# Rebuilding an attention core: transposed scores, row maxima one block ahead, every beat written out

## The reference

```
q, k, v = x @ Wq.T, x @ Wk.T, x @ Wv.T     # 32 query heads of 16, 16 key heads of 16, 8 value heads of 32
q, k = rope(q) * 16 ** -0.5, rope(k)       # each key head serves two query heads
probs = softmax(causal(q @ k.T))           # 32 maps of 1024 x 1024 for each sequence
diff = probs[even] - lambda * probs[odd]   # 16 differences; lambda from four small vectors
attn = rms_norm(diff @ v) * subln * (1 - LAMBDA_INIT)
x = x + attn @ Wo.T
h = gelu(layernorm(x) @ ternary(w1).T + b1)  # 512 -> 2048, weights -1, 0, 1
x = x + h @ ternary(w2).T + b2
```

## Time and profile before

| what | value |
| --- | --- |
| median of 3 runs | 4434.35 us (4434.32 to 4440.61) |
| span of the profiled execution | 4427.3 us |
| busy PE / DVE / ACT / POOL | 81 / 78 / 66 / 33% |
| HBM traffic | 106 MB read, 55 MB written |

### The profile page before, as it was taken

One profiled execution on the slowest core, in us unless ns is written; L12 is line 12 of the kernel. 1 busy time (PEld: TensorE's weight loads), 2 busy tenths in 40 slices (PEclk: granted clock), 3 DMA queues, 4 the chain that ended last, 5 costly groups with the idle time before them and its releaser, 6 DMA issues.

```text
span 4427.3 us, 80970 instructions
## 1 busy us (share of the span) xinstructions
PE 3604.6 (81%) x23454; PEld 2143.3 (48%) x23454; DVE 3467.0 (78%) x6124; ACT 2909.6 (66%) x6786; POOL 1450.2 (33%) x1563
## 2 busy tenths in 40 slices
PE   2688888888788887888878988888878888888886
PEld 1345544455444554544544544455544555444553
DVE  6778877888678886788867887678877788678891
ACT  1567756677566775667756766567666677567772
POOL 0233233332333333323343323433133332333323
PEclk7789989999899899998899988999989899899898
DMA  4212112211122112112122120222112121222110
GB/s 131 51 24 43 24 43 43 38 24 30 38 43 43 22 34 48 37 32 38 25 43 43 30 37 20 44 41 43 24 41 43 24 40 24 43 43 41 21 37 14
DMA packets 146768, 166.71 MB, mean 38 GB/s; under 512 B 16640, under 2 KB 117632, under 8 KB 145792
## 3 DMA queue, kind: packets, MB, share of 16 engines
q1 hardware_dynamic: 146304, 161.13, 18.0%
HBM read 105.95 MB, written 55.12 MB: 36 GB/s over the span
## 4 chain that ended last, share of the span: by engine, by line
PE 35%; DVE 28%; issue 22%; ACT 8%; DMA 3%; SPq 2%; POOL 2%; DVEq 1%; ACTq 0%; POOLq 0%
DVE NM L665 10%; PE M L867 6%; PE M L817 6%; PE F L889 5%; PE SP_ L832 5%; PE DP L844 5%; DVE E L689 4%; DVE CC L686 3%; PE F L902 3%; ACT E L541 2%; DMA KST<-scratch 2%; PE M L811 2%; ACT L541 2%; DVE RS L684 1%; DVE NM L673 1%
## 5 line engine op out<-in xcount | busy, mean ns | idle before, releaser
L541 ACT ACTIVATE E<-SP_,NM 128x256 f32<-128x256 f32 (+7 forms) x2048 | 1518.6, 743 | 733.6 <-DVE NM L665 526.4
L665 DVE TENSOR_REDUCE NM<-SP_ 128x1 f32<-128x896 f32 (+3 forms) x1024 | 1032.6, 1017 | 225.1 <-PE SP_ L833 222.9
L832 PE MATMUL SP_<-KST,QST 96*128 96x512 bf16 (+3 forms) x3072 | 864.1, 355 | 407.7 <-ACT E L541 345.5
L689 DVE SCALAR_TENSOR_TENSOR E<-E,CC 128x512 f32<-128x512 f32 (+7 forms) x1024 | 994.6, 971 | 36.1
L553 ACT ACTIVATE DT<-DP 128x512 f32<-128x512 f32 (+3 forms) x1024 | 527.8, 515 | 546.2 <-PE DP L844 524.0
L844 PE MATMUL DP<-ident,E 128*128 128x128 f32 x3328 | 614.5, 302 | 208.6 <-DVE E L689 207.3
L673 DVE TENSOR_REDUCE NM<-SP_ 128x2 f32<-128x1024 f32 (+3 forms) x512 | 419.8, 820 | 297.2 <-PE SP_ L833 290.3
L832 PEld LDWEIGHTS SP_<-KST,QST 96*128 96x128 bf16 x3072 | 278.7, 103 | 762.7 <-ACT E L541 537.1
L844 PEld LDWEIGHTS DP<-ident,E 128*128 128x128 f32 x3328 | 391.1, 153 | 382.2 <-issue 203.1
L889 PE MATMUL F<-X2H,W1Q 128*128 128x256 f16 x2048 | 502.0, 283 | 69.9 <-ACT HP L596 65.8
L817 PE MATMUL M<-WQKV,WT 128*128 128x512 f32 x1040 | 530.8, 607 | 8.4 <-DVE T L648 4.1
(11 more groups left out here) (86 smaller groups left out, 4780.3 us busy)
## 6 DMA issues: line engine op xcount, KB each, us to landing
QST<-scratch SPq DMA_DIRECT2D x390, 128.0 KB, 4.4
scratch<-SPL SPq DMA_DIRECT2D x65, 576.0 KB, 2.8
KST<-scratch SPq DMA_DIRECT2D x390, 64.0 KB, 5.0
X<-in_x SPq DMA_DIRECT2D x66, 256.0 KB, 3.1
out<-SQ SPq DMA_DIRECT2D x64, 256.0 KB, 2.1
KST<-in_w1T SPq DMA_DIRECT2D x1, 4096.0 KB, 19.2
DT<-in_w2T SPq DMA_DIRECT2D x1, 4096.0 KB, 28.7
WQKV<-in_wqT SPq DMA_DIRECT2D x1, 1024.0 KB, 7.3
```

Source lines behind the costliest of these rows:

```text
L541: act.activation(dst, score_out(i, 2 * n + k, w), ACT.Exp, bias=NM[:, (2 * u + k) % 8:(2 * u + k) % 8 + 1], scale=1.0, accum_out=SUM[:, i ...
L665: nc.vector.tensor_reduce(NM[:, m:m + 1], score_out(i, 2 * n + k, P * (i + 1)), AX.X, ALU.max, negate=True).then_inc(max_ready, 1)
L689: nc.vector.scalar_tensor_tensor(out=E1[:, u % 2, 0:w], in0=E2[:, e:e + w], scalar=CC[:, u % 2:u % 2 + 1], in1=E1[:, u % 2, 0:w], op0=ALU. ...
L832: pe.matmul(SP_[:, k[a // 512], 0:n], q, KST[0:ROWS, a // P:(a + n) // P, kk, :], start=True, stop=not last)
```

## The change

The attention core is written anew, and the order of work around it too.

- Scores are computed twice. `maxima` computes them with queries on the partitions, for the block after the current one (128 to 512 columns for each of two row halves of the array, 48 rows each), and VectorE reduces them to negative maxima, 152 reductions for each sequence of eight blocks. The maxima are turned by a transpose (`MT0`, `MT1`), cut to fp16 rows (`MROW`) and copied by eight small DMAs for each block into row 48 of `QST`; row 48 of `KST` holds ones. `scores_turned` then computes scores with keys on the partitions, with the negative maximum added by that row, in steps of eight heads (4 x 256 columns).
- ScalarE takes exp of 128 x 1024 in one instruction (`exps`), with no bias and no row sum. The result `PT` is already turned, and multiplies V directly (`weighted` on PE). Row sums come from a product with ones. There are 4 (t + 1) such steps for a block, in four phases.
- VectorE's `weighted` takes the reciprocal of 128 x 256 sums, multiplies, and forms the difference of the two maps after the V product, once for each phase.
- q and k are two fp16 parts with three products (48 rows) in place of three bf16 parts with six (96 rows). The projections are fp16 pairs: three fp16 matmuls in place of one f32.
- All work outside attention (projections, transposes, FFN products) goes through one bank `M`, one task for each of 16 beats of a block, with `m_full` and `m_free` as the only counters. First products: three pieces in odd blocks, five in even ones; second products: two in odd blocks. Projections run two blocks ahead, LN1 three.
- Nothing loops: all 64 blocks and 7 of start and tail are written out. The ternary weights are cut inside blocks -2 and 0.

```diff
-PROD = 6
-QPART = (0, 0, 0, 1, 1, 2)
-KPART = (0, 1, 2, 0, 1, 0)
+PROD = 3
+QPART = (0, 2, 1)
+KPART = (0, 1, 2)
+KEYS = 12
+BEATS = 16
+XT, AT, MT1, QP, KV, AN, QT, KT, WO_, MT0, X2T = 0, 2, 3, 4, 6, 8, 9, 11, 12, 13, 14
+FIRST_ODD, FIRST_EVEN = (1, 5, 7), (1, 5, 7, 10, 15)
+SECOND_ODD = (10, 15)
+SPLIT_ODD, SPLIT_EVEN = (1, 2, 6, 8), (6, 8, 9, 11)
+SQ_AT, MS_AT, POW_AT, MUL_AT = 3, 4, 5, 6
+ADD_Q, ADD_K, SPLIT_Q, SPLIT_K = 5, 7, 10, 12
+LN1_STATS, LN1_POW, LN1_ROWS = 10, 11, 15
+LN2_STATS, LN2_POW, LN2_ROWS = 12, 12, 13
+def group_at(n, k):
+    t = n % TILES
+    per = (t + 2) // 2
+    g = -(-k * 4 * per // BEATS)
+    if g >= 4 * per or g * BEATS // (4 * per) != k:
         return None
+    return g // per, 2 * (g % per), min(2 * (g % per) + 2, t + 1)
+def weighted_at(n, k):
+    m = n if k else n - 1
+    g = group_at(m, (k - 1) % BEATS)
+    return (m, *g) if g else None
+MAX_UNITS = (2, 4, 8, 8, 10, 12, 16, 16)
...
         @block.sync
...
+            def max_rows(n, u, blk, k):
+                m_taken(sp, blk, k)
+                for a in range(2):
+                    row = QST[64 * a + ROWS:64 * a + ROWS + 1, n % 3, :, :].rearrange("p (y c) n -> p y c n", c=4)
+                    for c2 in range(2):
+                        sp.dma_start(row[:, :, 2 * u + c2, :], MROW[8 * a + 4 * c2:8 * a + 4 * c2 + 4, u, :]).then_inc(rows_in[u], 16)
+            for n in range(-3, N + 4):
...
+                if tile(n + 2):
+                    stack_out(n + 2)
+                if tile(n + 1):
+                    max_rows(n + 1, 0, n, MT0)
+                if tile(n + 2):
+                    stack_in(n + 2)
...
         @block.scalar
...
+            def exps(n, ph, j0, j1):
+                for j in range(j0, j1):
+                    s = steps_before(n) + ph * (n % TILES + 1) + j
+                    after(act, st_full, s + 1)
+                    after(act, pv_done, s - 3)
+                    act.activation(PT[:, s % 4, :], STB[:, 2 * (s % 2):2 * (s % 2) + 2, :].rearrange("p a n -> p (a n)"),
+                                   ACT.Exp).then_inc(e_done, 1)
...
         @block.vector
...
+                after(dve, s_full, units_before(n, u) + i + 1)
+                nc.vector.tensor_reduce(dst, SB[:, :, 0:c * w].rearrange("p a (c w) -> p a c w", c=c), AX.X, ALU.max,
+                                        negate=True).then_inc(s_free, 1)
...
+            def weighted(n, ph):
+                f = 4 * n + ph
+                after(dve, pv_done, steps_before(n) + (ph + 1) * (n % TILES + 1))
+                nc.vector.reciprocal(RS[:, :], A[:, 2 * P:4 * P]).then_inc(inv_ready, 1)
+                after(dve, inv_ready, f + 1)
+                nc.vector.tensor_tensor(OD[:, :], A[:, 0:2 * P], RS[:, :], ALU.mult).then_inc(a_free, 1)
+                after(dve, a_free, f + 1)
+                nc.vector.scalar_tensor_tensor(out=ATC[:, n % 2, ph, :], in0=OD[:, P:2 * P], scalar=neglam[:, 0:1], in1=OD[:, 0:P],
+                                               op0=ALU.mult, op1=ALU.add).then_inc(at_ready, 1)
...
         @block.tensor
...
+                for j in range(j0, j1):
+                    s = steps_before(n) + ph * (t + 1) + j
+                    after(pe, e_done, s - 1)
+                    for c2 in range(2):
+                        for a in range(2):
+                            r = slice(64 * a, 64 * a + ROWS + 1)
+                            ins = pe.matmul(STB[:, 2 * (s % 2) + a, 256 * c2:256 * c2 + 256],
+                                            KST[r, (n - t + j) % KEYS, 2 * (2 * c2 + h2) + u, :],
+                                            queries(n)[r, 2 * h2:2 * h2 + 2, 2 * u + c2, :],
+                                            start=(c2 == 0), stop=(c2 == 1 and j < t), skip_group_check=True)
...
+                    after(pe, e_done, s + 1)
+                    if j == 0:
+                        after(pe, a_free, 4 * n + ph)
+                    for part in range(2):
+                        for c2 in range(2):
+                            for a in range(2):
+                                g = 2 * c2 + a
+                                v = DV * (4 * u + g)
+                                left = ones[:, 0:DV] if part else V[:, (n - t + j) % KEYS, v:v + DV]
+                                ins = pe.matmul(A[DV * g:DV * g + DV, 256 * part:256 * part + 256], left,
+                                                PT[:, s % 4, 512 * a + 256 * c2:512 * a + 256 * c2 + 256],
+                                                start=(part == 0 and j == 0), stop=(j == t), skip_group_check=True)
...
+            def maxima(n, u, i):
+                if u == 0 and i == 0:
+                    after(pe, stacked, STACK * (n + 1))
+                after(pe, s_free, units_before(n, u) + i)
+                for e in range(c):
+                    c2, y = divmod(e0 + e, 4)
+                    for a in range(2):
+                        r = slice(64 * a, 64 * a + ROWS)
+                        k1 = (n - t + k0) % KEYS
+                        ins = pe.matmul(SB[:, a, w * e:w * e + w], queries(n)[r, y, 2 * u + c2, :],
+                                        KST[r, k1:k1 + kt, 2 * (2 * c2 + y // 2) + u, :], start=(e == 0),
+                                        stop=(e == c - 1 and not diagonal), skip_group_check=True)
...
+            def project(high, low, wh, wl, c0):
+                for j in range(KD):
+                    c = slice(P * j, P * (j + 1))
+                    pe.matmul(M[:, :], high[:, c], wh[:, j, c0:c0 + D], start=(j == 0), stop=False)
+                    pe.matmul(M[:, :], high[:, c], wl[:, j, c0:c0 + D], start=False, stop=False)
+                    ins = pe.matmul(M[:, :], low[:, c], wh[:, j, c0:c0 + D], start=False, stop=(j == KD - 1))
+                ins.then_inc(m_full, 1)
...
+            for n in range(-3, N + 4):
+                for k in range(BEATS):
+                    if group_at(n, k):
+                        scores_turned(n, *group_at(n, k))
+                    u, units = units_at(n + 1, k)
+                    for i in units[:1]:
+                        maxima(n + 1, u, i)
+                    if weighted_at(n, k):
+                        weighted(*weighted_at(n, k))
+                    for i in units[1:]:
+                        maxima(n + 1, u, i)
+                    if (n, k) not in M_AT:
+                        continue
+                    after(pe, m_free, M_AT[n, k])
+                    if k == XT:
+                        after(pe, xn_ready, n + 3)
+                        turn(XN, KD)
...
+                    elif first_piece(n, k):
+                        after(pe, cut_done, 2)
+                        first_product(*first_piece(n, k))
+                    elif second_piece(n, k):
+                        second_product(*second_piece(n, k))
```

More of the change, by code:

```diff
@@ L169, in every_block @@
-def every_block(eng, run):
-    for t in range(TILES):
-        run(QBlock(0, t, "first"))
-    with eng.Fori(1, B) as b:
-        for t in range(TILES):
-            run(QBlock(b, t, "loop"))
-    for t in range(3):
-        run(QBlock(B, t, "last"))
+AS, WS = 32.0, 256.0
+PS = 1.0 / (AS * WS)
+LOW = 64.0
+PROD = 3
+QPART = (0, 2, 1)
+KPART = (0, 1, 2)
+ROWS = PROD * DH
+STACK = 4 * PROD * 16
+KEYS = 12
+BEATS = 16
+CUT = 1024
+XT, AT, MT1, QP, KV, AN, QT, KT, WO_, MT0, X2T = 0, 2, 3, 4, 6, 8, 9, 11, 12, 13, 14
@@ new lines, in joins_before, with units_before, units_at, unit @@
+def joins_before(n):
+    b, t = divmod(n, TILES)
+    return b * 8 + 2 * max(0, t - 4)
+MAX_UNITS = (2, 4, 8, 8, 10, 12, 16, 16)
+ABREAST = (4, 2, 1, 1)
+def units_before(n, u):
+    b, t = divmod(max(0, min(n, N)), TILES)
+    return b * 2 * sum(MAX_UNITS) + 2 * sum(MAX_UNITS[:t]) + u * MAX_UNITS[t]
+def units_at(n, k):
+    if not tile(n):
+        return 0, range(0)
+    c = MAX_UNITS[n % TILES]
+    u, k = divmod(k, 8)
+    return u, range(-(-k * c // 8), -(-(k + 1) * c // 8))
+def unit(t, i):
+    if t < 4:
+        return i * ABREAST[t], ABREAST[t], 0, t + 1, 0
+    if i < 8:
+        return i, 1, 0, 4, 0
+    return (i - 8) * ABREAST[t - 4], ABREAST[t - 4], 4, t - 3, 1
@@ new lines, in hidden_split @@
+            def hidden_split(m, p):
+                f = slice(2 * p, 2 * p + 2)
+                after(pool, gelu_done, 2 * m + p // 4 + 1)
+                if m and p == 0:
+                    after(pool, m_full, M_AT[2 * m + 3, SECOND_ODD[1]] + 1)
+                pool.tensor_scalar(HH[:, f, :], HP[:, f, :], 1.0, 0.0, ALU.mult, ALU.add).then_inc(h_chain, 1)
+                after(pool, h_chain, 8 * m + p + 1)
+                pool.tensor_tensor(HL[:, f, :], HP[:, f, :], HH[:, f, :], ALU.subtract).then_inc(h_ready, 1)
@@ L821, in scores @@
-            def scores(b, i, s):
-                w = P * (i + 1)
-                k = banks(i, s)
-                if s == 0:
-                    after(pe, stacked, 16 * 2 * PROD * (b * TILES + i + 1))
-                after(pe, exp_done, b * N_E + SLOT_FREE[i * NQ + s])
```

(9 more changed lines are left out.)

1219 lines of the change are left out of this document (535 added, 684 removed).

## The result

The kernel with the change takes 4962.5 us (median; 4960.4 to 4964.1) against 4436.1 of the kernel before in the same rounds: 1.118 times the time, 95% interval 1.117 to 1.120. It is slower by 526 us; 4320 was forecast, with 3990 to 4800 as the range, so the time lies outside the range, and the kernel became slower where faster was forecast.

A forecast was written before the change was run, and what follows sets the result against it. PE was to set the pace: 449 us of own work a sequence plus 60 of waits and 6 of clock, 518 with rounding against 532.8; 4427.3 - 8 x 14.8 = 4309, stated as 4320, range 3990 to 4800.

The forecast's parts named there:

- all three lie under PE's 449: Per sequence, ScalarE 255, VectorE 318 and GpSimd 150 us lie under PE's own work of 449, which sets the pace.
- the list of waits: Per sequence: bank M 26, DMA of stacked Q and K 21, Gelu before exps 13, sum 60; clock 6.
- Reciprocal, 0.42: VectorE, end of each phase: reciprocal of 128x256 row sums priced like a product, 0.42 us, 32 times a sequence.
- rival B: Reciprocal at 1.4 us or more delays V product and reduction: 16 to 32 us, 4450 to 4570 us; chance 0.16.
- Rival A: Row halves of turned scores and maxima don't run together on PE: 70 us a sequence, time 4880; chance 0.16.
- C: The waits hide, PE at work 0.93 of its time: waits 30 us, clock full, period 479, time 4010; chance 0.2.
- D: Waits above 75 us (DMA wait every block, cold clock in even ones): period 530 to 550, 4415 to 4570; chance 0.13.
- PE's own prices: Per sequence: scores 38, second scores 31, masks 15, V products 144, projections 62, FFN 111, transposes 22, form changes 26.
- Wait (1): Tasks sharing the one PSUM bank M wait for the last one's readers: 26 us a sequence, mostly in short blocks.
- The clock, 6: Granted clock 1.00 except 0.92 in blocks t=0 and t=2, costing 6 us a sequence.
- Start and tail: Time outside the loop of eight sequences: 165 us before, no change within 20 forecast.
- What ScalarE and VectorE save: Per sequence ScalarE falls from 364 to 255 us, VectorE from 427 to 318; about 2050 and 2550 in all.

The follow-up runs named there:

- the one with two banks: Changed kernel without the second score product and its reductions, tasks of bank M alternating between M and a former maxima bank: 4000.6 us, ratio 0.903.

## Why the prediction was wrong

**The step that failed** is the sentence "So all three lie under PE's 449, and what ScalarE and VectorE save is worth nothing beyond that", and with it the list of waits, which has four and none for the maxima's banks. VectorE's total does lie under PE's (340 against 489 us busy a sequence). But SB is one pair of banks: PE can't fill it while VectorE reduces it, and two units of a beat follow each other directly in PE's queue. Any time between filling and freeing is PE's idle time unless other PE work lies between. PE's waits came to 103 us a sequence in place of 60, and 54 of them (354.9 + 77.2 over the run) are for these banks. Price of the reductions so exposed: 40 us a sequence (maxima over fewer elements). A sum of busy times can't show it; the number of buffers between two engines and what stands between two uses in the queue would have.

**Reciprocal, 0.42.** Mis-sized, at 1.75. It is rival B, whose condition (1.4 or more) came true. Its price of 16 to 32 a sequence was a little low: 35 measured. Its time of 4450 to 4570 missed because the reductions' 40 came on top. Cut together, the two bring the period from 594 to 521, next to the forecast 518. Of the two places that B named, the reduction that stands behind the reciprocal is the one that counts; the wait of the next V product (A <- DVE OD) is 23.3 us over the whole run. The choice of 0.42 was made from rows that could not decide (128x2 in 159 ns), against the Trainium skill's paragraph on the iterative divide (VectorE: DVE Perf Modes, why there are eight slices), which pointed the right way.

**Rival A** fell: row halves run together, 0.225 a step. It named a time of 4880 near the measured one, for a reason that the timeline excludes. **C** fell as well. **D** had the right kind, waits above 75, but named the DMA and the clock; the DMA's part is 14.5 a sequence. Shortening it by 12 us over the run gave 4 us in the full kernel, less than can be told, and taking it away gave 27 in the one with two banks.

**PE's own prices** held one by one: 0.21 for a 512-column product, 0.225 for a turned step, 0.89 for a step of V products. Their sum of 449 was not measured by itself. The run with both of VectorE's parts cut agrees with it: 466 us busy at 0.95 of the clock, 521 in all. That 521 and 518 are so near is luck in part, since the clock took more there than the 6 forecast (some 24 by its 0.95, an estimate: 449 / 0.95 - 449) and the waits less than the 60.

**Wait (1), the single bank M, 26.** Too small at least where it could be tried: 50 a sequence with no second products. In the full kernel the maxima use both banks of SB, so there it was not tried.

**The clock, 6.** Forecast 1.00 but for t=0 and 2; the windows say 0.91 over the sequence, 0.86 to 0.90 in the first five stretches and 0.94 to 0.98 in the last three. With the reciprocal cut, a third of the gain (90 of 281) is PE's busy time at a faster clock. The forecast priced the clock as a term of its own; it comes with the waits.

**Start and tail.** Forecast as 165 us, with no change within 20; measured 4958.7 - 8 x 593.9 = 207. So 42 of the 526 us are not in the loop. No run cuts them apart; with both of VectorE's parts cut they are 180.

**What ScalarE and VectorE save** was right in size: DVE 2797 (2550 forecast; the reciprocals alone cost 340 more), ACT 1822 (2050).

**Left open:** whether a second pair of banks for the maxima would hide the reductions in the full kernel; which of the waits in the short blocks (stretches one, two and eight, 54 us of the 144 left over) could go in the full kernel; why the task between the two maxima made the kernel slower; and how much of the 50 us of the second task bank is wait and how much clock.

## What to carry to other kernels

Before summing busy times, list every buffer that two engines hand back and forth, count its copies, and put next to each what its reader does first when it comes free: with one copy, reader and writer add up. An engine's cut is worth what it takes out of such hand-overs: the same narrower V product gave 120, 333 and 481 us as they went away, and the same reciprocal 281, 243 and 85. When an operation that no row shows lies in such a hand-over, take the dear end of its range as its price, and try the operation by itself first.

## What the runs showed of the hardware

- A reciprocal of 128x256 f32 from PSUM took 1753 ns and one of 128x2 159 ns: (1753 - 159) / 254 = 6.3 ns an element, as an estimate that takes the time to grow evenly with the width. It took four times as long as a product of that size (424).
- Two matmuls on 48 or 49 rows each, in two row halves and two banks, ran in the time of one: 0.225 us for four of 256 columns, where one by one they would take 4 x 0.109.
- The granted clock was lower where PE waited more, also in short waits: with 318 waits of some 1.1 us for the maxima it was 0.897 over the run, without the reciprocal 0.921, with both of VectorE's parts cut 0.940. With 460 us less work of PE and 495 such waits it was 0.818.
